# Two edits on the TensorE path of a post-LN transformer layer: V transposes emitted one group later, output bias added as two bf16 rows

## What is computed

```python
def attn(x, w_qkv, b_qkv, w_out, b_out):
    qkv = einsum('bsh,oh->bso', x, w_qkv) + b_qkv
    q, k, v = split(qkv, 3, axis=-1)
    probs = softmax(einsum('bqh,bkh->bqk', q, k) / sqrt(2048))
    context = einsum('bqk,bkh->bqh', probs, v)
    return einsum('bsh,oh->bso', context, w_out) + b_out
def ternarize(w):                    # q in {-1,0,1} by |w| > 0.7 * mean|w|
    return q * abs_mean
def ffn(x, w_fc, w_proj):            # hidden size 5120
    h = square(relu(x @ ternarize(w_fc).T))
    return h @ ternarize(w_proj).T
x = layernorm(x + attn(x, ...))
x = layernorm(x + ffn(x, ...))
```

## Time and profile before

| | us |
|---|---|
| median of the 2 runs shown | 7868.86 (7792.02 and 7945.71) |
| profiled execution, its own time | 7788.81 |
| span of its slowest core (core 7) | 7787.2 |
| spans of the eight cores | 7732.9 to 7787.2 |
| mean granted TensorE clock by core | 0.924 to 0.932 of 2.4 GHz |

### The profile page before, as it was taken

How to read it: one execution, slowest core, us unless ns; L and a number is a source line. 1 busy time by engine, 2 the same in 40 slices (tenths; PEclk the granted TensorE clock), 3 DMA queues, 4 the chain that set the end, 5 groups by cost and what they waited for, 6 DMA issues and landing times.

```text
span 7787.2 us, 82314 instructions; the slowest of 8 cores (7732.9 to 7787.2 us)
## 1 busy us (share of the span) xinstructions
PE 6826.1 (88%) x29840; PEld 3018.8 (39%) x29840; DVE 1319.4 (17%) x2407; ACT 1550.6 (20%) x2522; POOL 258.0 (3%) x498
## 2 busy tenths in 40 slices
PE   5999999998998798899779789977979998797998
PEld 2444443444443343334334333433433443343343
DVE  3111344211110201210110211011021000202101
ACT  3444666412221101210110111011021000102100
POOL 0111222100000000000000000000000000000000
PEclk9999998999999798899879799987979998797999
DMA  3667777423333132122313212231312223131222
GB/s 102 180 188 194 219 236 233 149 63 85 87 87 102 59 118 74 45 67 76 117 60 117 62 55 68 75 121 59 116 49 65 69 73 129 59 113 46 65 69 83
DMA packets 394272, 785.58 MB, mean 101 GB/s; under 512 B 105105, under 2 KB 219793, under 8 KB 381585
## 3 DMA queue, kind: packets, MB, share of 16 engines
q1 hardware_dynamic: 334994, 570.59, 23.4%
q0 software_dynamic: 58880, 209.75, 9.4%
HBM read 654.34 MB, written 125.83 MB: 100 GB/s over the span
## 4 chain that ended last, share of the span: by engine, by line
PE 74%; ACT 9%; DVE 7%; DMA 4%; issue 4%; SPq 1%; DVEq 0%; ACTq 0%; POOL 0%; POOLq 0%
PE pb L436 17%; PE pb L912 14%; PE pb L972 14%; PE pb L625 9%; PE pb L807 8%; PE pb L736 8%; DVE ab L271 2%; ACT af L265 2%; ACT af L269 2%; DMA ab<-qfc 1%; SPq L61 1%; PE pb L818 1%; DMA af<-wot 1%; ACT af L855 1%; PE pb L327 1%
## 5 line engine op out<-in xcount | busy, mean ns | idle before, releaser
L436 PE MATMUL pb<-ab,ab 128*128 128x512 bf16 x9216 | 2078.6, 389 | 34.5 <-ACT af L269 27.1
L436 PEld LDWEIGHTS pb<-ab,ab 128*128 128x128 bf16 x9216 | 919.5, 100 | 1168.4 <-issue 244.7
L912 PE MATMUL pb<-ab,ab 128*128 128x512 bf16 x5120 | 1171.7, 388 | 112.2 <-DMA ab<-qfc 105.5
L972 PE MATMUL pb<-ab,ab 128*128 128x512 bf16 x5120 | 1115.1, 380 | 18.6 <-DVE ab L927 11.3
L912 PEld LDWEIGHTS pb<-ab,ab 128*128 128x128 bf16 x5120 | 495.6, 99 | 787.5 <-issue 279.7
L625 PE MATMUL pb<-ab,ab 128*128 128x512 bf16 x3072 | 674.8, 383 | 140.5 <-DMA ab<-qf 139.4
L972 PEld LDWEIGHTS pb<-ab,ab 128*128 128x128 bf16 x5120 | 499.8, 98 | 634.0 <-issue 44.8
L807 PE MATMUL pb<-ab,ab 128*128 128x512 bf16 x3072 | 682.4, 386 | 28.4 <-DMA ab<-wos 14.4
L736 PE MATMUL pb<-ab,ab 128*128 128x512 bf16 x3072 | 670.4, 382 | 4.6 <-DVE ab L694 4.6
L625 PEld LDWEIGHTS pb<-ab,ab 128*128 128x128 bf16 x3072 | 302.6, 99 | 512.5 <-issue 159.6
L807 PEld LDWEIGHTS pb<-ab,ab 128*128 128x128 bf16 x3072 | 303.9, 99 | 411.0 <-issue 61.2
(11 more groups left out here) (84 smaller groups left out, 2574.9 us busy)
## 6 DMA issues: line engine op xcount, KB each, us to landing
af<-wfct POOLq DMA_DIRECT2D x160, 512.0 KB, 5.3
af<-wprt POOLq DMA_DIRECT2D x160, 512.0 KB, 6.1
ab<-qfc SPq DMA_DIRECT2D x640, 128.0 KB, 3.0
ab<-qpr SPq DMA_DIRECT2D x320, 256.0 KB, 2.6
ab<-kf SPq DMA_DIRECT2D x128, 512.0 KB, 3.3
ab<-vt SPq DMA_DIRECT2D x128, 512.0 KB, 3.3
ab<-wos SPq DMA_DIRECT2D x128, 512.0 KB, 3.5
af<-wqk SPq DMA_DIRECT2D x48, 1024.0 KB, 7.1
```

The lines of the kernel that those rows point to most:

```text
L436: t_mm = B.op("tensor", lambda e, a=a, bmat=bmat, hc=hc, ss=ss, bk=bk, first=first, last=last: e.matmul(pb[bk], a[:, hc * 128:(hc + 1) * 128],
L912: t_mmf[bk] = B.op("tensor", lambda e, dc=dc, h4=h4, amat=amat, bk=bk, first=first, last=last: e.matmul(pb[bk], qfcs[:, dc * 512 + h4 * 12 ...
L972: t_last = B.op("tensor", lambda e, a_ap=a_ap, sci=sci, qpb=qpb, ds=ds, bk=bk, first=first, last=end_of_acc: e.matmul(pb[bk], a_ap[:, sci ...
```

## The change

Two independent edits.

1. V transposes. The code after the staging copy (transposes, hi, lo, two DMAs) becomes a function `v_emit`, and each group's call is put off until the next group's matmuls and staging copy have been appended. The last group's call comes after the loop. The number of instructions is the same.
2. Output bias. At the start `bout` is loaded into the first x row buffer, split once into `bout_hi` and `bout_lo` (one ScalarE activation, one VectorE subtraction), and the first x load waits for that subtraction. Each of the 64 f32 bias matmuls becomes two bf16 matmuls with a bf16 row of ones.

```diff
     t_b1 = B.dma(bqkv_sb, bqkv_in[:, :], stream="b0")
-    t_b2 = B.dma(bout_sb, bout_in[:, :], stream="b1")
+    bout_stage = bf(131072, 2048)[0:1, :]
+    t_b2 = B.dma(bout_stage, bout_in[:, :], stream="b1")
+    B.op("gpsimd", lambda e: e.memset(ones_bf, 1.0), inc="sG")
+    t_bh = B.op("scalar", lambda e: e.activation(bout_hi, bout_stage, AF.Copy),
+                waits=[t_b2], inc="sA")
+    t_bl = B.op("vector", lambda e: e.tensor_tensor(bout_lo, bout_stage, bout_hi,
+                                                    op=AL.subtract),
+                waits=[t_b2, t_bh], inc="sV")
...
         t_ld = B.dma(xrow, x_in[sci * 128:(sci + 1) * 128, :],
-                     waits=[prev_row[sci % 2]], stream="xr%d" % (sci % 2))
+                     waits=[prev_row[sci % 2], t_bl if sci == 0 else None],
+                     stream="xr%d" % (sci % 2))
...
+    def v_emit(oc, ss, bk, ei, t_cp):
+        hcv = oc - 32
...
+        for j in range(4):
+            t_trs.append(B.op("tensor", lambda e, bk=bk, j=j, vstg=vstg: e.matmul(
+                pb[bk][:, j * 128:(j + 1) * 128], vstg[:, j * 128:(j + 1) * 128],
+                idn, start=(j == 0), stop=(j == 3), is_transpose=True),
+                waits=[t_cp] if j == 0 else (), inc="sP" if j == 3 else None))
...
                 t_cp = B.op("scalar", lambda e, bk=bk, vstg=vstg: e.copy(
                     vstg, pb[bk]),
                     waits=[t_mm, vstg_free[ei]] +
                     (tern_final if oc == 32 and ss < 2 else []), inc="sA")
-                t_trs = []
...
-                bank_free[bk] = t_last_lo
+                pend = v_pending.pop(0) if v_pending else None
+                v_pending.append((oc, ss, bk, ei, t_cp))
+                if pend is not None:
+                    v_emit(*pend)
...
+    for pend in v_pending:
+        v_emit(*pend)
+    v_pending = []
     for _ in tern_it:
         pass
...
+                B.op("tensor", lambda e, bk=bk, boff=boff: e.matmul(
+                    pb[bk], ones_bf, bout_hi[:, boff:boff + 512],
+                    start=False, stop=False), waits=[t_bh, t_g0] if g == 0 and oh == 0 and bk == 0 else ())
                 t_bias = B.op("tensor", lambda e, bk=bk, boff=boff: e.matmul(
-                    pb[bk], ones_row, bout_sb[:, boff:boff + 512],
-                    start=False, stop=True), waits=[t_b2], inc="sP")
+                    pb[bk], ones_bf, bout_lo[:, boff:boff + 512],
+                    start=False, stop=True), waits=[t_bl] if g == 0 and oh == 0 and bk == 0 else (), inc="sP")
```

More of the change, by code:

```diff
@@ L134, in build_core @@
     ones_row = nc.alloc_sbuf_tensor("ones_row", [1, 128], F32).ap()
-    bout_sb = nc.alloc_sbuf_tensor("bout_sb", [1, 2048], F32).ap()
+    ones_bf = nc.alloc_sbuf_tensor("ones_bf", [1, 128], BF16).ap()
+    bout_hi = nc.alloc_sbuf_tensor("bout_hi", [1, 2048], BF16).ap()
+    bout_lo = nc.alloc_sbuf_tensor("bout_lo", [1, 2048], BF16).ap()
     bqkv_sb = nc.alloc_sbuf_tensor("bqkv_sb", [128, 48], F32).ap()
@@ L415, in build_core @@
     vt4 = vt.rearrange("(kc hh p) c -> kc hh p c", hh=2, p=128)
+    v_pending = []
+    def v_emit(oc, ss, bk, ei, t_cp):
+        hcv = oc - 32
+        hh, pos = hcv // 8, (hcv % 8) * 128
+        vstg = bf(VSTG[ei], 512)
+        ei4 = (oc * 4 + ss) % 4
+        tf = tern_final if oc == 32 else []
+        vehw = bb(VEH[ei4], 512)
+        velw = bb(VEL[ei4], 512)
+        t_trs = []
+        for j in range(4):
[3 more added lines that the diff above has]
+                waits=[t_cp] if j == 0 else (), inc="sP" if j == 3 else None))
+        t_his = None
+        for j in range(4):
+            t_his = B.op("scalar", lambda e, bk=bk, j=j, vehw=vehw: e.activation(
+                vehw[:, j * 128:(j + 1) * 128],
+                pb[bk][:, j * 128:(j + 1) * 128], AF.Copy),
+                waits=([t_trs[3], veh_free[ei4]] + tf) if j == 0 else (),
+                inc="sA" if j == 3 else None)
+        t_last_lo = None
+        for j in range(4):
+            t_last_lo = B.op("vector", lambda e, bk=bk, j=j, vehw=vehw, velw=velw: e.tensor_tensor(
+                velw[:, j * 128:(j + 1) * 128],
+                pb[bk][:, j * 128:(j + 1) * 128],
+                vehw[:, j * 128:(j + 1) * 128], op=AL.subtract),
+                waits=([t_trs[3], t_his, vel_free[ei4]] + tf) if j == 0 else (),
+                inc="sV" if j == 3 else None)
+        dst_hi = vt4[ss * 4:ss * 4 + 4, hh, :, pos:pos + 128].transpose([1, 0, 2])
+        dst_lo = vt4[ss * 4:ss * 4 + 4, hh, :, 1024 + pos:1024 + pos + 128].transpose([1, 0, 2])
+        veh_free[ei4] = B.dma(dst_hi, vehw, waits=[t_his], stream="vh%d" % ei4)
+        vel_free[ei4] = B.dma(dst_lo, velw, waits=[t_last_lo], stream="vl%d" % ei4)
+        vstg_free[ei] = t_trs[3]
+        bank_free[bk] = t_last_lo
     qk_load(0)
@@ L470, in build_core @@
                 hcv = oc - 32
-                hh, pos = hcv // 8, (hcv % 8) * 128
+                ei = (oc * 4 + ss) % 2
                 vstg = bf(VSTG[ei], 512)
```

## The result

| | before | changed | ratio |
|---|---|---|---|
| executions at the usual clock, changed against before | | | 0.9835, 95% interval 0.9777 to 0.9892 |
| median of all executions shown, us | 8288.53 (10) | 7855.11 (12) | |
| lowest, us | 7792.02 | 7663.81 | |
| profiled execution, its own time, us | 7788.81 | 7727.33 | |

The forecast was 7665 us, a gain of 1.6%, in a range of 7627 to 7743. The ratio, 1.65% less, is close to what was forecast; its interval reaches to both sides of 2%, so whether the gain is above 2% is not decided. The median of 7855.11 lies outside the range. Seven of the ten executions of the kernel before and six of the twelve of the changed one lie 2 to 14% above the lowest of their kernel, with a lower mean clock on the cores of one die or of both wherever the cores were recorded, and the medians above contain them.

The account below looks back on a forecast made before the run. TensorE was taken to set the time; -86 (V) - 33 (oh = 0) - 13 (oh = 1) + 7 (start) + 1 (stage end) = -124 us on 7788.81 gave 7665 us, range 7627 to 7743.

Parts of the forecast that it names:

- What bounds the kernel: Whole kernel: TensorE sets the time, so an edit is worth what it takes out of TensorE's own sequence.
- V edit, -86 + 1: V groups: 63 of 64 waits for the staging copy go, saving 86 us; the stage's end costs 1 us.
- Rival B: V groups: gaps go but exposed weight loads or late ScalarE splits limit the gain to 57 us; 7694 us, chance 18%.
- D: V groups: the V edit does nothing because transposes still wait for the copy; 7751 us, chance 1%.
- the `kf` load at T + 15.5: End of stage 3: first `kf` load 15.5 us after the last V group's matmuls end (T), before T + 14.7.
- Clock in the V groups: V groups: made as dense as the q/k groups, they keep a granted clock of 1.00.
- Rival C: V groups: without gaps the chip grants less clock there, priced at 0.81; slower, 7820 us, chance 4%.
- Bias, oh = 0, -33: Four oh = 0 bias blocks: 3.43 us of bf16 matmuls replace 9.66 us plus a 2.0 us slow tail, saving 33 us.
- rival A: oh = 0 bias blocks: the clock still falls in the short blocks, gain 25 us instead of 33; 7673 us, chance 17%.
- oh = 1, -13: Four oh = 1 bias blocks before layer norm: 7.0 us instead of 10.24 each, saving 13 us, between 8 and 15.
- Start, +7: Program start: the first x load waits for the `bout` load and split, costing 7 us, between 4 and 10.
- The sum, -124: Whole kernel: all terms together take 124 us off the profiled 7788.81 us, giving 7665 us.

Follow-up runs that it names:

- e7: e3 without bias matmuls, VectorE adding the bias to the residual, last V group emitted before the last `wos` unit; median span 7589.0 us (cores 4 to 7).
- e1: The V edit alone, bias as in the kernel before; median span of die 0 7659.0 us, 88 us less than before.
- e2: The bias edit alone, V transposes in the order of the kernel before; median span of die 0 7723.5 us, 23.5 us less than before.
- e3: The changed kernel with `bout` loaded and split among the V groups instead of at the start; median span of die 0 7619.8 us, 12.6 us less.
- e4: e3 with the bias matmuls on 128 rows instead of one; the part behind the V groups took 5265.7 us instead of 5277.6.
- e6: e3 with every one-row bias matmul done twice; the part behind the V groups took 5319.1 us.
- e5: e3 with the bias matmuls streaming a row of the probabilities instead of the bias; clock fell at 23 of 32 blocks, no time given.
- e10: The changed kernel with the first four ternary-weight loads held until the first x block landed; q/k groups start at 214.3 us instead of 216.7.
- e8: The kernel of e2 executed once more, for the spread; median span of die 0 7726.9 us.

## Why the prediction was right, and where it was wrong

**What bounds the kernel: right.** What was taken out of TensorE's sequence came off the span nearly in full (in e7 some 30 of 40 us), and what was put into the start chain was added: e1 and e2 add up to within 4 us of both together, and e3 gets back the 10 us of the start.

**V edit, -86 + 1: right.** -83 on cores 0 to 3, -88 on core 7, whose rows were used. The period of 10.85 was 10.79: the switch between kinds of matmul, costed at 0.09 between 0 and 0.2, is 0.03. No wait took the gaps' place. Both figures hold also what chance does to the q and k groups. Rival B (63 x 0.9) and D are refuted by the 670.8 us, on cores 0 to 3 here and on all eight in e1; the `kf` load at T + 15.5 came as worked out.

**Clock in the V groups, "I take 1.00": right for this comparison.** 1.00 in every stretch of them on core 0; cores 4 and 5 had 0.97 to 0.99, but were low long before the V groups began. Rival C, that the edit itself lowers the clock, is refuted by e1: its V groups take 670.8 us at clock 1.00 on all eight cores.

**Bias, oh = 0, -33: mechanism right, one step wrong.** The step that failed is "Does the clock still fall? ... I take no fall". It fell in or behind 22 of 32 blocks; rival A, to which I gave 17%, is what mostly happened. The step rests on one block, the first of core 7, where the clock fell 4.5 us in. The same trace has 32 of them, and the first slow weight load stands 2.3 to 6.0 us behind the start, in four of them within 3.4. The first block of core 0, which begins at 2942.55:

```profile
2944.37 0.18 PEld L818 LDWEIGHTS pb<-bout_sb,ones_row 1*128 1x128 f32 x1 [0.24 <-issue]
2944.80 0.33 PEld L818 LDWEIGHTS pb<-bout_sb,ones_row 1*128 1x128 f32 x1 [0.25 <-issue]
```

So "over before the fall" could not hold for every block. The other half of the error is that a block that is over in time does not save the clock either: mostly the fall comes in the dense matmuls behind it. e4 shows that it is the one row, e6 that longer one-row work makes it certain, e5 that zeros have no part. From oh = 0 to oh = 1 are 7.1 us less per group (95.0 to 88.0): 28 us where the forecast had 33, and 25 for rival A.
**oh = 1, -13: about right.** The block takes 2948.23 - 2941.20 = 7.03 us, as worked out; from one such block to the next group's first 2.1 us are saved in the changed kernel and 2.7 to 4.3 in the four others with the same bias, 8 to 17 us in all, where 13 was forecast. Both parts together were -40, e1 against e3 -41, forecast -46.

**Start, +7: too small.** It was +9.8. Two terms were mis-sized: `bout` took 2.8 us where I took the 1.6 us of the `bqkv` row, and the x load, now issued behind four weight loads, took 8.7 us where the row of before had 7.2. e10 shows that the weight loads cost this load about 2 us and the whole start 2.4. I had moved the load past GpSimd's queue and had not counted what stood in it; that is within the given 4 to 10, but the reason was missed.

**The sum, -124: -115 by cores 0 to 3, 0.9835 by ratio.** The errors are +5 in the clock of oh = 0, +3 in the start, +1 to 3 in V. That the ratio of 1.65% comes out nearer to the 1.6% forecast than these parts do (115 of 7747 us, 1.5%) is luck: its interval is over 1% wide, and three errors of one sign lie under it.

**The range: wrong, and this is the step that failed against the measured time.** "The range is the two ends of the sum with 0.3% (23 us) for the spread between executions." The two executions shown lay 2% apart, I said so, and then took the lower one as the base and 0.3% as the spread. Of the 22 executions in the table of the result 13 lie 2 to 14% above the lowest of their kernel, and so the median of 7855.11 is 112 us above the upper end of 7743. An execution of e7 shows in one profile what this is, two cores at the same time in the V groups, core 0 and core 2:

```profile
1900.00:1950.00 50.00, 50.00 (x200) 22.04 (x199) 8.14 (x18) 8.22 (x22) 0.00 (x0) 0.81 0.36 100
```

```profile
1900.00:1950.00 50.00, 49.74 (x239) 23.98 (x242) 9.52 (x20) 12.49 (x28) 0.00 (x0) 1.00 0.31 85
```

Core 0 is granted 0.81 and passes 200 where core 2 passes 239.

I had weighed the rule of the Trainium skill (TensorE: Matmul & The Clock Gate, Part 1: dense matmuls on three or more cores of a die are held at 13/16) against one row, clock 1.00 on core 7, and written that the trace does not agree. 13/16 is 0.8125, and the same trace has it on the same core in short stretches of the q and k groups, 46 of them with 316 us in all by its clock records. One of them:

```profile
521.20:529.50 8.30, 8.30 (x33) 3.46 (x32) 2.45 (x2) 3.46 (x4) 0.83 (x2) 0.81 0.90 239
```

All eight cores of the kernel before have such stretches: over the whole span 45 to 60 us on cores 0 to 3, which is at most 11 us of lost time (60 x 0.19, an estimate), and 319 to 347 us on cores 4 to 7. The profiles of e1 to e6 and of the repeat e8 have none on any core. So the rule agrees with some stretches and some executions and not with others, in e7 not even with all cores of a die at once; Since the kernel before has it and e1 has not, it is no effect of the V edit. As the spread between executions it had its place in the range. What decides whether a core is held in an execution stays open.

## What to carry to other kernels

Where an engine's queue is strictly in order, a round trip to another engine (here TensorE, ScalarE's copy, TensorE again) cost nothing once the second half was emitted one unit later; look for idle time before the same line once per unit, and check what the later emission is now queued behind. Price an addition to the start of a program with every queue that it is moved past, since transfers of other queues come first then; better, move such work to a stage in which its engines idle, as e3 did. Where the trace holds a place many times, as the 32 bias blocks here, read them all before a moment is taken from one. And take the spread of a range from all executions shown, not from the profiled one.

## What the runs showed of the hardware that I had not expected

- One-row matmuls let the clock fall from the 2.4 to the 1.2 GHz level while they run without a gap: 0 of 32 blocks of oh = 0 with 128 rows, 19 to 23 of 32 with one row and 3.4 us (six executions), 32 of 32 with one row and 6.9 us. The fall comes inside the block or, mostly, after it is over, in dense full matmuls (4.9 us after its start in the rows above).
- A one-row f32 matmul of 512 columns takes TensorE as long as four one-row bf16 ones (95.0 us from block to block in the kernel before and in e6).
- ScalarE and VectorE take as long for one row of 2048 elements as for 128 rows (1.91 and 2.28 us; 1.91 and 2.29 in the earlier trace rows).
